# The norms of x on TensorE: turned blocks, squared from PSUM and summed by matmuls with a column of ones

## The chip, the cores and the metric

The kernel runs on one core of a Trainium2 chip. The metric is the device time of one execution, in microseconds (us); a smaller number is better.

## What is computed

The input x has 4096 rows of 128 numbers, and adj is a 4096 x 4096 matrix of zeros and ones. The first layer needs the norm of each row of x, the cosines between all rows, a softmax over them masked by adj, and two products with x; then come a layer norm, a second product with adj, a weight matrix, and another layer norm. The part that the change touches is the norm:

```python
norms = jnp.maximum(jnp.linalg.norm(x, axis=-1), COS_EPS)
sim = x @ x.T / (norms[:, None] * norms[None, :])
attn = jax.nn.softmax(beta * sim * adj, axis=1)
...
return diffusion + jax.nn.sigmoid(alpha) * (attn @ x - x)
```

## The kernel before

The rows of x are held as 32 blocks of 128 rows (`x_keep`), loaded by four DMAs of 512 KB, each a quarter q of eight blocks (L238). Then SyncE's queue issues the pieces of adj (L242), and casts of them on ScalarE (L482) free their buffers again.

The opening of the program makes the unit rows, each row of x divided by its norm, turned so that the row's 128 numbers lie across the partitions. For a quarter q the steps are:

- ScalarE squares the quarter's numbers. Quarters 0 to 2 take one instruction each (`squares`, L457). Quarter 3 takes eight, one per block, and each of these also sums its own squares (`block_squares`, L467).
- VectorE sums the squares of quarters 0 to 2 (L655) and takes the larger of the sum and a floor (`norms2`, L658).
- ScalarE takes the root (`norm_root`, L474), VectorE the reciprocal (`rnorm`, L664).
- GpSimd multiplies the quarter by its reciprocals (`unit_rows`, L313), one quarter after another.
- TensorE transposes the unit rows, four blocks at a time (`turn_rows`, L991, eight groups g). ScalarE writes the upper half of each as fp16 (`turned_high`, L490), VectorE the rest (`xnt_low`, L668).

From all norms VectorE finds the largest in each partition (L681); TensorE turns that column (L1084), VectorE finds the largest of all (L689), TensorE spreads it to all partitions by a matmul with a column of ones (L1087), and VectorE makes scales of it (L692 to L695). GpSimd waits for these scales before it splits x into fp16 parts (`x_split`, L359).

Then the cosines start (L1007). Row blocks r = 0 to 31 follow, in a loop from r = 2 on: cosines on TensorE, masking with adj on VectorE (L708), exponentials on ScalarE (L523), transposes of them (L1018), products with x (L1040, L1043). The second part sums y and z with adj on TensorE (L1056, L1176, L1204).

Everything is written by hand: each engine has its own program, in which instructions run in the order written, and semaphores tie the engines together. TensorE's program of the opening is the list of calls from L1075 on. In it, `keep_busy(n)` issues n matmuls of the identity with itself, whose results nobody reads:

```python
keep_busy(24)
...
turn_rows(0)
turn_rows(1)
keep_busy(3)
turn_rows(2)
turn_rows(3)
keep_busy(5)
```

An fp32 matmul appears in the trace as two passes, each with a weight load and a matmul record; an fp32 transpose appears as one.

Of the kernel before, what the change touches and what calls it, by code (L numbers as in the profile page):

```python
# [26 lines left out]
ALU = mybir.AluOpType  # L27
ACT = mybir.ActivationFunctionType
AX = mybir.AxisListType
F32 = mybir.dt.float32  # L30
# [7 lines left out]
P = 128  # L38
# [10 lines left out]
MIN_NORM = 1e-8  # L49
# [3 lines left out]
def two_layer_gnn(nc, x, adj, alpha, beta, weights, out):  # L53
    N, D = x.shape
    R = N // P
# [3 lines left out]
    CH = 1024  # L59
    C = N // CH  # L60
    TC = CH // P
    H = N // BANK
    TH = BANK // P
# [11 lines left out]
    with ExitStack() as ctx:  # L75
        def sb(name, shape, dt):
            return ctx.enter_context(nc.sbuf_tensor(name, shape, dt))

        def psum(name, shape, dt):
            return ctx.enter_context(nc.psum_tensor(name, shape, dt))  # L80

        def sem(name):
            return ctx.enter_context(nc.semaphore(name))
# [5 lines left out]
        x_keep = sb("x_keep", [P, R, D], F32)  # L89
# [6 lines left out]
        u = sb("u", [P, R, D], F32)  # L96
# [3 lines left out]
        ident = sb("ident", [P, P], F32)  # L100
        col = sb("col", [P, 30], F32)
        packed = sb("packed", [P, 2, W], U32)
        norm2 = sb("norm2", [P, R, 2], F32)
        norm = sb("norm", [P, R], F32)
        norm_r = sb("norm_r", [P, R], F32)
        deg = sb("deg", [P, C, R], F32)
# [9 lines left out]
        def c(n):  # L116
            return col[:, n:n + 1]
        alpha_c, beta_c, e_alpha, sigma, _, abs_beta = (c(n) for n in range(6))
        neg_max = [c(6), c(29)]
        total, r_total, gain = (c(n) for n in range(7, 10))  # L120
        attn_scale, x_up, dif_scale, _, _, eps_c = (c(n) for n in range(10, 16))
        great, pow2, rpow2 = c(16), c(18), c(20)
        sign_beta, top = c(24), c(25)
        table_loads = [c(26), c(27), c(28)]
        rstd = sb("rstd", [P, G], F32)

        ps_s = psum("ps_s", [P, 2, BANK], F32)
        ps_e = psum("ps_e", [P, 4, BANK], F32)
        ps_acc = psum("ps_acc", [P, BANK], F32)
        ps_at = psum("ps_at", [P, BANK], F32)  # L130

        x_loaded = [sem(f"x_loaded{q}") for q in range(C)]
# [3 lines left out]
        land_full = [[sem(f"land_full{q}_{i}") for i in range(C)] for q in range(2)]  # L136
        ident_zero = sem("ident_zero")
        ident_done = sem("ident_done")
        squares_done = sem("squares_done")
        norms2_done = sem("norms2_done")  # L140
        root_done = sem("root_done")
        floor_set = sem("floor_set")
        dve_step = sem("dve_step")
        rnorm_done = sem("rnorm_done")
        xn_done = [sem(f"xn_done{q}") for q in range(C)]
# [69 lines left out]
        zT = late[:, 0:2 * BANK].rearrange("p (a i) -> p a i", a=2)  # L215
        early = scores[:, 1, :]
        zw_ps = [ps_acc, ps_at]
        attn_ps = [ps_acc[:, :], ps_e[:, 3, :]]
        sum_ps = [ps_s[:, 0, :], ps_s[:, 1, :], ps_e[:, 2, :], ps_e[:, 3, :]]
        ones = eT_parts[0:1, 1, 1, 0:2 * P].bitcast(F32)  # L220
# [81 lines left out]
        @block.gpsimd  # L302
        def _(pool):
            nc.gpsimd.memset(ones, 1.0)
            nc.gpsimd.memset(ident[:, :], 0.0).then_inc(ident_zero, 1)
            pool.wait_ge(ident_zero, 1)
            nc.gpsimd.affine_select(out=ident[:, :], in_=ident[:, :], compare_op=ALU.not_equal, fill=1.0, base=0,
# [144 lines left out]
        @block.scalar  # L452
        def _(act):

            def squares(q):
                act.wait_ge(x_loaded[q], 16)
                nc.scalar.activation(early[:, q * CH:(q + 1) * CH],  # L457
                                     x_keep[:, q * TC:(q + 1) * TC, :].rearrange("p r d -> p (r d)"),
                                     ACT.Square).then_inc(squares_done, 1)

            def block_squares(q, a):

                if a == 0:
                    act.wait_ge(floor_set, 1)
                    act.wait_ge(x_loaded[q], 16)
                for r in range(q * TC + a * TC // 2, q * TC + (a + 1) * TC // 2):
                    ins = nc.scalar.activation(early[:, r * P:(r + 1) * P], x_keep[:, r, :], ACT.Square,  # L467
                                               accum_out=norm2[:, r, 0:1])
                if a == 1:
                    ins.then_inc(squares_done, 1)  # L470

            def norm_root(q):
                act.wait_ge(norms2_done, q + 1)
                nc.scalar.activation(norm[:, q * TC:(q + 1) * TC], norm[:, q * TC:(q + 1) * TC], ACT.Sqrt,  # L474
                                     scale=1.0 / (XN_SCALE * XN_SCALE)).then_inc(root_done, 1)
# [12 lines left out]
            def turned_high(g):  # L488
                act.wait_ge(xnt_turned, g + 1)
                nc.scalar.activation(xn_parts[:, 0, g * BANK:(g + 1) * BANK], ps_e[:, g % 4, :],  # L490
                                     ACT.Copy).then_inc(xnt_hi, 1)

            squares(0)
            squares(1)
            norm_root(0)
            squares(2)
            norm_root(1)
            block_squares(3, 0)
            turned_high(0)
            norm_root(2)  # L500
            block_squares(3, 1)
            turned_high(1)
            norm_root(3)
            turned_high(2)
# [132 lines left out]
        def _(dve):  # L637
            steps = [0]

            def link(ins):  # L640

                steps[0] += 1
                ins.then_inc(dve_step, 1)
                dve.wait_ge(dve_step, steps[0])
# [1 line left out]
            nc.vector.memset(eps_c, LN_EPS).then_inc(eps_set, 1)  # L646

            nc.vector.memset(top, 0.0)
            nc.vector.memset(norm2[:, :, 1:2], MIN_NORM * MIN_NORM).then_inc(floor_set, 1)

            def norms2(q):

                dve.wait_ge(squares_done, q + 1)
                if q < C - 1:
                    link(nc.vector.tensor_reduce(norm2[:, q * TC:(q + 1) * TC, 0],  # L655
                                                 early[:, q * CH:(q + 1) * CH].rearrange("p (r d) -> p r d", d=D),
                                                 AX.X, ALU.add))
                nc.vector.tensor_reduce(norm[:, q * TC:(q + 1) * TC], norm2[:, q * TC:(q + 1) * TC, :], AX.X,  # L658
                                        ALU.max).then_inc(norms2_done, 1)

            def rnorm(q):

# [312 lines left out]
        def _(pe):  # L975
            pe.wait_ge(ident_done, 1)
            def keep_busy(n):

                for _ in range(n):
                    nc.tensor.matmul(ps_acc[:, 0:P], ident[:, :], ident[:, :], start=True, stop=True)  # L980

            keep_busy(24)

            def turn_rows(g):

                pe.wait_ge(xn_done[g // 2], 1)
                if g >= 4:
                    pe.wait_ge(xnt_lo, g - 3)
                for n in range(TH):
                    t = TH * g + SLOT[n]  # L990
                    ins = nc.tensor.transpose(ps_e[:, g % 4, n * P:(n + 1) * P], early[:, t * P:(t + 1) * P],  # L991
                                              ident[:, :])
                ins.then_inc(xnt_turned, 1)
# [67 lines left out]
            def row(r, q, second=False):  # L1061

                for h in range(H):
# [8 lines left out]
                    else:  # L1072
                        attend(r - 1, 1 - q, h + H - LAG, second, order=range(H) if second else ATTEND_ORDER)

            turn_rows(0)  # L1075
            turn_rows(1)
            keep_busy(3)
            turn_rows(2)
            turn_rows(3)
            keep_busy(5)  # L1080
            turn_rows(4)
            turn_rows(5)
            pe.wait_ge(great_done, 1)
# [4 lines left out]
                             start=True, stop=True).then_inc(great_spread, 1)  # L1088
# [165 lines left out]
```

## Time and profile before

| what | us |
|---|---|
| median of 3 runs | 655.35 |
| lowest and highest run | 654.85, 655.55 |
| the profiled execution's own time | 654.72 |
| its span, first to last instruction | 652.9 |
| TensorE busy | 638.8 (98% of the span) |
| VectorE busy | 516.7 (79%) |
| ScalarE busy | 412.6 (63%) |
| GpSimd busy | 237.4 (36%) |

The span is 1.8 us shorter than the execution's own time, which also holds what lies around the first and last instruction. Busy time counts all stretches together. The change lies in the first 18 us, and what TensorE's program does there is seen in the timeline and not in the shares.

### The profile page before, as it was taken

How to read it: one execution, taken by the hardware profiler on the slowest of the kernel's cores; microseconds unless marked ns; L12 is line 12 of the kernel's file. 1: busy time of each engine (PE TensorE's matmuls, PEld its weight loads, DVE VectorE, ACT ScalarE, POOL GpSimd, SP SyncE). 2: the span in 40 equal slices, each digit the busy share in tenths (PEclk: the TensorE clock that was granted, in tenths of full speed). 3: DMA queues.
4: the chain of work that ended last, by engine and by line, in shares of the span. 5: the costliest groups of instructions: out<-in, count | busy, mean ns of one | idle time of the engine just before them, and what ended most of it. 6: DMA issues, size and time to landing. Idle time of an engine off the chain costs nothing.

```text
span 652.9 us, 16141 instructions
## 1 busy us (share of the span) xinstructions
PE 638.8 (98%) x5103; PEld 465.8 (71%) x5103; DVE 516.7 (79%) x1565; ACT 412.6 (63%) x768; POOL 237.4 (36%) x249
## 2 busy tenths in 40 slices
PE   8889999999999999999999999999999999999996
PEld 7456777777777777777777777888888864444465
DVE  5989999999999999999999998887777863334453
ACT  7999999999999999999999998611111110000000
POOL 5999644544544544644644647300000000000000
PEclk9999999999999999999999999999999999999999
DMA  7879999999999999999999995300000000000001
GB/s 278 310 162 256 298 236 246 289 252 244 292 251 234 297 247 251 306 241 248 299 239 251 289 252 95 73 7 0 0 0 0 0 1 1 17 16 18 16 32 33
DMA packets 165020, 107.37 MB, mean 164 GB/s; under 512 B 144384, under 2 KB 148608, under 8 KB 164992
## 3 DMA queue, kind: packets, MB, share of 16 engines
q1 hardware_dynamic: 164992, 107.04, 62.7%
q8 instruction: 12, 0.20, 0.1%
q14 instruction: 16, 0.13, 0.1%
HBM read 69.27 MB, written 2.10 MB: 109 GB/s over the span
## 4 chain that ended last, share of the span: by engine, by line
PE 90%; DVE 3%; ACT 2%; DMA 2%; issue 1%; POOL 1%; SPq 0%; DVEq 0%; ACTq 0%; POOLq 0%
PE ps_s L1007 23%; PE ps_s L1204 17%; PE ps_e L1176 15%; PE ps_acc L1040 8%; PE ps_e L1018 8%; PE ps_e L1040 8%; PE ps_acc L1043 4%; PE ps_e L1043 4%; DMA x_keep<-in_x 1%; DMA eTx<-e_parts 1%; DVE scores L708 1%; PE ps_e L1056 1%; ACT scores L523 1%; DVE y_parts L819 1%; PE ps_s L1056 1%
## 5 line engine op out<-in xcount | busy, mean ns | idle before, releaser
L1007 PE MATMUL ps_s<-xn_parts,xn_signed 128*128 128x512 f16 x756 | 203.3, 379 | 2.9 <-DVE cmax L708 2.9
L708 DVE CUSTOM_DVE_ANT_1 scores<-ps_s,adj_bytes 128x512 f32<-128x512 f32 x252 | 171.8, 684 | 22.3 <-PE ps_s L1007 15.3
L523 ACT ACTIVATE scores<-scores,col 128x1024 f32<-128x1024 f32 x128 | 157.3, 1232 | 1.1 <-DVE col L719 0.9
L482 ACT ACTIVATE adj_bytes<-land 128x1024 uint8<-128x1024 f32 x128 | 133.5, 1047 | 0.6 <-POOL packed L343 0.6
L351 POOL TENSOR_SCALAR e_parts<-scores 128x1024 f16<-128x1024 f32 x64 | 68.5, 1071 | 152.9 <-ACT scores L523 149.4
L1176 PE MATMUL ps_e<-y_parts,stage 128*128 128x256 f16 x896 | 98.0, 273 | 0.0
L1007 PEld LDWEIGHTS ps_s<-xn_parts,xn_signed 128*128 128x128 f16 x756 | 68.5, 98 | 38.5 <-DVE cmax L708 2.5
L1176 PEld LDWEIGHTS ps_e<-y_parts,stage 128*128 128x128 fp8e4 x896 | 87.7, 98 | 10.1
L530 ACT ACTIVATE eT_parts<-ps_e 128x512 f16<-128x512 f32 x128 | 75.9, 596 | 26.2 <-PE ps_e L1018 25.0
L723 DVE SCALAR_TENSOR_TENSOR eT_parts<-ps_e,eT_parts 128x512 f16<-128x512 f32 x128 | 87.3, 684 | 1.9 <-ACT eT_parts L530 1.9
L729 DVE SCALAR_TENSOR_TENSOR e_parts<-scores,e_parts 128x1024 f16<-128x1024 f32 x64 | 86.3, 1350 | 0.4 <-POOL e_parts L351 0.4
L1018 PE MATMUL ps_e<-ident,scores 128*128 128x128 f32 x512 | 77.0, 274 | 0.8 <-ACT scores L523 0.8
L619 ACT ACTIVATE scores<-ps_s 128x512 f32<-128x512 f32 (+1 forms) x9 | 4.9, 550 | 108.6 <-PE ps_s L1204 108.6
L596 ACT ACTIVATE std<-mv,col 128x1 f32<-128x1 f32 x32 | 9.4, 295 | 84.2 <-DVE mv L900 84.2
L1204 PE MATMUL ps_s<-stage,x_parts 128*128 128x512 fp8e4 (+1 forms) x320 | 56.9, 336 | 0.0
L1204 PE MATMUL ps_s<-land,x_parts 128*128 128x512 fp8e4 x256 | 56.4, 379 | 0.0
L1018 PEld LDWEIGHTS ps_e<-ident,scores 128*128 128x128 f32 x512 | 53.9, 140 | 3.0 <-DVE eT_parts L723 0.8
L805 DVE TENSOR_SCALAR stage<-packT 128x256 uint32<-128x256 uint32 (+1 forms) x192 | 42.6, 286 | 12.5 <-PE ps_e L1176 12.3
L1040 PE MATMUL ps_acc<-x_parts,eT_parts 128*128 128x256 f16 x256 | 49.1, 273 | 1.6 <-DVE eT_parts L723 1.6
L340 POOL TENSOR_TENSOR packed<-packed,adj_bytes 128x256 uint32<-128x256 uint32 x48 | 49.4, 1029 | 2.7
L1040 PE MATMUL ps_acc<-x_parts,eTx 128*128 128x256 f16 x256 | 48.9, 273 | 0.5 <-DMA eTx<-e_parts 0.5
L1040 PE MATMUL ps_e<-x_parts,eT_parts 128*128 128x256 f16 x256 | 48.9, 273 | 0.0
(128 smaller groups left out, 972.2 us busy)
## 6 DMA issues: line engine op xcount, KB each, us to landing
land<-in_adj SPq DMA_DIRECT2D x128, 512.0 KB, 5.4
x_keep<-in_x SPq DMA_DIRECT2D x4, 512.0 KB, 5.6
out<-u SPq DMA_DIRECT2D x7, 256.0 KB, 2.1
eTx<-e_parts SPq DMA_TRANSPOSE x64, 4.3
packT<-packed SPq DMA_TRANSPOSE x16, 7.0
out<-u SPq DMA_DIRECT2D x2, 128.0 KB, 1.7
scores<-in_L_gnn_weights SPq DMA_DIRECT2D x1, 64.0 KB, 1.9
col<-in_L_gnn_beta SPq DMA_DIRECT2D x1, 0.5 KB, 7.2
```

The costliest lines, as they stand in the source:

```text
L351: nc.gpsimd.tensor_scalar(e_parts[:, n, 0, :], scores[:, q, (n + 2) * CH:(n + 3) * CH], E_SCALE, 1.0, ALU.mult, ALU.mult).wait_op(sign_don ...
L482: nc.scalar.activation(adj_bytes[:, q, i * CH:(i + 1) * CH], land[:, q, i, :], ACT.Copy, scale=float(BYTE_TOP[q] >> i), accum_out=deg[:, i ...
L523: nc.scalar.activation(piece, piece, ACT.Exp, bias=neg_max[q], scale=abs_beta, accum_out=csum[:, q, i:i + 1]).then_inc(exp_done, 1)
L530: nc.scalar.activation(eT_parts[:, b, 0, :], ps_e[:, b % 2, :], ACT.Copy, scale=E_SCALE).then_inc(e_hi, 1)
L708: nc.vector.tensor_tensor_reduce(scores[:, q, o:o + BANK].rearrange("p (k q) -> p k q", k=K), score_bank(h, r == 0 if start else False).re ...
L723: nc.vector.scalar_tensor_tensor(eT_parts[:, b, 1, :], ps_e[:, b % 2, :], E_SCALE, eT_parts[:, b, 0, :], ALU.mult, ALU.subtract).then_inc( ...
L729: nc.vector.scalar_tensor_tensor(e_parts[:, n, 1, :], scores[:, q, (n + 2) * CH:(n + 3) * CH], E_SCALE, e_parts[:, n, 0, :], ALU.mult, ALU ...
L1007: ins = nc.tensor.matmul(score_bank(h, start), xn_signed[:, q, part, :], xn_parts[:, other, o:o + BANK], start=(part == 0 and other == 0), ...
L1018: ins = nc.tensor.transpose(ps_e[:, b % 2, n * P:(n + 1) * P], scores[:, q, t * P:(t + 1) * P], ident[:, :])
L1040: nc.tensor.matmul(attn_ps[q][:, 0:2 * D], hi, x_parts[:, t, :], start=(k == 0 and n == 0), stop=(k == H - 1 and n == TH - 1), skip_group_ ...
L1176: ins = nc.tensor.matmul(ps_e[:, n, 0:2 * D], stage8[n][:, b, :, k], y_tiles[t], start=(t == 0), stop=(t == R - 1))
L1204: ins = nc.tensor.matmul(ps_s[:, q, 0:rows * P], x_parts[:, t, part * D:(part + 1) * D], quads8[q if rows == G else 1][:, b, k, n:n + rows ...
```

## The change

The squares of x are no longer taken from x itself. TensorE transposes the raw blocks of x, four at a time, into PSUM (`turn_raw`); ScalarE squares the turned blocks from PSUM into `u` (`raw_squares`); TensorE multiplies each squared block with a column of ones, which sums over the partitions and leaves the squared norms of 128 rows as one column in PSUM (`sum_norms`); VectorE only takes the larger of sum and floor (`norms2`). VectorE's sums and ScalarE's eight single blocks of quarter 3 go, as does the table of floors. The column of ones is set by GpSimd at the start. Eight groups g of four blocks replace the four quarters of the squares. `keep_busy` falls from 24 to 8 at the start, and calls of 2, 2, 3 and 3 stand between the new steps.

```diff
...
-        norm2 = sb("norm2", [P, R, 2], F32)
...
+        one = c(13)
...
+        one_set = sem("one_set")
+        raw_turned = sem("raw_turned")
+        norms_summed = sem("norms_summed")
-        floor_set = sem("floor_set")
...
+        norm_ps = ps_at[:, 3 * P:3 * P + R]
...
+            nc.gpsimd.memset(one, 1.0).then_inc(one_set, 1)
...
         @block.scalar
         def _(act):
-            def squares(q):
-                act.wait_ge(x_loaded[q], 16)
-                nc.scalar.activation(early[:, q * CH:(q + 1) * CH],
-                                     x_keep[:, q * TC:(q + 1) * TC, :].rearrange("p r d -> p (r d)"),
+            def raw_squares(g):
+
+                act.wait_ge(raw_turned, g + 1)
+                nc.scalar.activation(u[:, TH * g:TH * g + TH, :].rearrange("p n d -> p (n d)"), ps_s[:, g % 2, :],
                                      ACT.Square).then_inc(squares_done, 1)
-
-            def block_squares(q, a):
-
-                if a == 0:
-                    act.wait_ge(floor_set, 1)
-                    act.wait_ge(x_loaded[q], 16)
-                for r in range(q * TC + a * TC // 2, q * TC + (a + 1) * TC // 2):
-                    ins = nc.scalar.activation(early[:, r * P:(r + 1) * P], x_keep[:, r, :], ACT.Square,
-                                               accum_out=norm2[:, r, 0:1])
-                if a == 1:
-                    ins.then_inc(squares_done, 1)
             def norm_root(q):
                 act.wait_ge(norms2_done, q + 1)
...
                 nc.scalar.activation(xn_parts[:, 0, g * BANK:(g + 1) * BANK], ps_e[:, g % 4, :],
                                      ACT.Copy).then_inc(xnt_hi, 1)
-            squares(0)
-            squares(1)
+            raw_squares(0)
+            raw_squares(1)
+            raw_squares(2)
             norm_root(0)
-            squares(2)
+            raw_squares(3)
             norm_root(1)
-            block_squares(3, 0)
+            raw_squares(4)
+            raw_squares(5)
             turned_high(0)
             norm_root(2)
-            block_squares(3, 1)
+            raw_squares(6)
+            raw_squares(7)
             turned_high(1)
             norm_root(3)
             turned_high(2)
...
             nc.vector.memset(eps_c, LN_EPS).then_inc(eps_set, 1)
             nc.vector.memset(top, 0.0)
-            nc.vector.memset(norm2[:, :, 1:2], MIN_NORM * MIN_NORM).then_inc(floor_set, 1)
             def norms2(q):
-                dve.wait_ge(squares_done, q + 1)
-                if q < C - 1:
-                    link(nc.vector.tensor_reduce(norm2[:, q * TC:(q + 1) * TC, 0],
-                                                 early[:, q * CH:(q + 1) * CH].rearrange("p (r d) -> p r d", d=D),
-                                                 AX.X, ALU.add))
-                nc.vector.tensor_reduce(norm[:, q * TC:(q + 1) * TC], norm2[:, q * TC:(q + 1) * TC, :], AX.X,
-                                        ALU.max).then_inc(norms2_done, 1)
+                dve.wait_ge(norms_summed, q + 1)
+                nc.vector.tensor_scalar(norm[:, q * TC:(q + 1) * TC], norm_ps[:, q * TC:(q + 1) * TC],
+                                        MIN_NORM * MIN_NORM, None, ALU.max).then_inc(norms2_done, 1)
             def rnorm(q):
...
                 for _ in range(n):
                     nc.tensor.matmul(ps_acc[:, 0:P], ident[:, :], ident[:, :], start=True, stop=True)
-            keep_busy(24)
+            keep_busy(8)
+
+            def turn_raw(g):
+
+                pe.wait_ge(x_loaded[g // 2], 16)
+                if g >= 2:
+                    pe.wait_ge(squares_done, g - 1)
+                for n in range(TH):
+                    ins = nc.tensor.transpose(ps_s[:, g % 2, n * P:(n + 1) * P], x_keep[:, TH * g + n, :], ident[:, :])
+                ins.then_inc(raw_turned, 1)
+
+            def sum_norms(g):
+
+                if g == 0:
+                    pe.wait_ge(one_set, 1)
+                if g >= 2:
+                    pe.wait_ge(norms2_done, g // 2)
+                pe.wait_ge(squares_done, g + 1)
+                for t in range(TH * g, TH * g + TH):
+                    ins = nc.tensor.matmul(norm_ps[:, t:t + 1], u[:, t, :], one, start=True, stop=True)
+                if g % 2 == 1:
+                    ins.then_inc(norms_summed, 1)
             def turn_rows(g):
...
                     else:
                         attend(r - 1, 1 - q, h + H - LAG, second, order=range(H) if second else ATTEND_ORDER)
+            turn_raw(0)
+            turn_raw(1)
+            keep_busy(2)
+            sum_norms(0)
+            turn_raw(2)
+            sum_norms(1)
+            turn_raw(3)
+            keep_busy(2)
+            sum_norms(2)
+            sum_norms(3)
+            keep_busy(3)
+            turn_raw(4)
+            turn_raw(5)
             turn_rows(0)
             turn_rows(1)
-            keep_busy(3)
+            sum_norms(4)
+            sum_norms(5)
+            turn_raw(6)
+            turn_raw(7)
             turn_rows(2)
             turn_rows(3)
-            keep_busy(5)
+            sum_norms(6)
+            sum_norms(7)
+            keep_busy(3)
             turn_rows(4)
             turn_rows(5)
             pe.wait_ge(great_done, 1)
...
```

TensorE's program, before, from its first matmul to the last transposes of unit rows (L980 is `keep_busy`, L991 `turn_rows`, L1084 and L1087 the turning and the spreading of the largest norm):

```order
L980 MATMUL ps_acc<-ident 128x128 x24
L991 MATMUL ps_e<-ident,scores 128x128 x8
L980 MATMUL ps_acc<-ident 128x128 x3
L991 MATMUL ps_e<-ident,scores 128x128 x8
L980 MATMUL ps_acc<-ident 128x128 x5
L991 MATMUL ps_e<-ident,scores 128x128 x8
L1084 MATMUL ps_at<-ident,col 1x128
L980 MATMUL ps_acc<-ident 128x128 x3
L1087 MATMUL ps_at<-col,eT_parts 128x1
L991 MATMUL ps_e<-ident,scores 128x128 x8
```

The four quarters of unit rows are the only work here besides the filler and the largest norm.

The same place in the changed program, first half (L971 is `keep_busy`, L981 `turn_raw`, L992 `sum_norms`, L1003 `turn_rows`):

```order
L971 MATMUL ps_acc<-ident 128x128 x8
L981 MATMUL ps_s<-ident,x_keep 128x128 x8
L971 MATMUL ps_acc<-ident 128x128 x2
L992 MATMUL ps_at<-col,u 128x1 x4
L981 MATMUL ps_s<-ident,x_keep 128x128 x4
L992 MATMUL ps_at<-col,u 128x1 x4
L981 MATMUL ps_s<-ident,x_keep 128x128 x4
L971 MATMUL ps_acc<-ident 128x128 x2
L992 MATMUL ps_at<-col,u 128x1 x8
L971 MATMUL ps_acc<-ident 128x128 x3
L981 MATMUL ps_s<-ident,x_keep 128x128 x8
L1003 MATMUL ps_e<-ident,scores 128x128 x8
```

The first transposes of unit rows (L1003), which stood right behind the filler, now stand behind six groups of raw transposes and four groups of sums.

And the second half, to the turning of the largest norm (L1114, before L1084):

```order
L992 MATMUL ps_at<-col,u 128x1 x8
L981 MATMUL ps_s<-ident,x_keep 128x128 x8
L1003 MATMUL ps_e<-ident,scores 128x128 x8
L992 MATMUL ps_at<-col,u 128x1 x8
L971 MATMUL ps_acc<-ident 128x128 x3
L1003 MATMUL ps_e<-ident,scores 128x128 x8
L1114 MATMUL ps_at<-ident,col 1x128
```

The sums of quarter 3 are the last L992 row, behind the unit rows of quarter 1, which stand in the second L1003 row counting from the top.

ScalarE, before, from its first squares to the last root (L457 and L467 are squares, L474 roots, L490 `turned_high`):

```order
L457 ACTIVATE scores<-x_keep 128x1024 x2
L474 ACTIVATE norm<-norm 128x8
L457 ACTIVATE scores<-x_keep 128x1024
L474 ACTIVATE norm<-norm 128x8
L467 ACTIVATE scores,norm<-x_keep 128x128 x4
L490 ACTIVATE xn_parts<-ps_e 128x512
L474 ACTIVATE norm<-norm 128x8
L467 ACTIVATE scores,norm<-x_keep 128x128 x4
L490 ACTIVATE xn_parts<-ps_e 128x512
L474 ACTIVATE norm<-norm 128x8
```

and with the change (L462 is `raw_squares`, L467 the root, L483 `turned_high`):

```order
L462 ACTIVATE u<-ps_s 128x512 x3
L467 ACTIVATE norm<-norm 128x8
L462 ACTIVATE u<-ps_s 128x512
L467 ACTIVATE norm<-norm 128x8
L462 ACTIVATE u<-ps_s 128x512 x2
L483 ACTIVATE xn_parts<-ps_e 128x512
L467 ACTIVATE norm<-norm 128x8
L462 ACTIVATE u<-ps_s 128x512 x2
L483 ACTIVATE xn_parts<-ps_e 128x512
L467 ACTIVATE norm<-norm 128x8
```

Each L462 row reads PSUM that a `turn_raw` has written, so ScalarE's squares now wait for TensorE instead of a DMA.

## Rows read from the trace of the kernel before

**Rows 1.** The chain that ended last, 2 to 18 us: start, us, what.
```profile
2.31 7.44 DMA x_keep<-in_x
9.84 1.28 ACT scores L467 x8
...
11.70 1.17 ACT scores L467 x8
...
16.64 1.02 PE ps_e L991 x8
```
**Rows 2.** Busy time by stretch, all engines: PE, PEld, DVE, ACT, POOL, PEclk, DMA share, GB/s.
```profile
17.50:55.00 37.50, 32.26 (x228) 19.92 (x225) 34.19 (x89) 35.84 (x66) 35.56 (x38) 1.00 0.83 234
60.00:400.00 340.00, 339.99 (x2887) 249.36 (x2885) 316.61 (x821) 317.36 (x556) 176.14 (x189) 1.00 1.00 258
```
**Rows 3.** Timeline: start us, us, engine line op [idle before]; GpSimd, ScalarE, VectorE around the norms.
```profile
7.37 1.90 POOL L313 TENSOR_TENSOR scores<-x_keep,norm_r 128x1024 f32<-128x1024 f32 x1 [5.76 <-DVE norm_r L664]
12.02 3.75 POOL L313 TENSOR_TENSOR scores<-x_keep,norm_r 128x1024 f32<-128x1024 f32 x2 [0.21 <-DVE norm_r L664]
17.55 1.12 POOL L359 TENSOR_SCALAR u<-x_keep,col 128x1024 f32<-128x1024 f32 x1 [0.64 <-DVE col L695]
...
13.48 0.20 DVE L664 RECIPROCAL norm_r<-norm 128x8 f32<-128x8 f32 x1 [0.41 <-ACT norm L474]
...
4.29 1.06 ACT L457 ACTIVATE scores<-x_keep 128x1024 f32<-128x1024 f32 x1 [2.06 <-DMA x_keep<-in_x]
6.63 0.17 DVE L658 TENSOR_REDUCE norm<-norm 128x8 f32<-128x16 f32 x1
6.83 0.21 ACT L474 ACTIVATE norm<-norm 128x8 f32<-128x8 f32 x1
7.08 0.20 DVE L664 RECIPROCAL norm_r<-norm 128x8 f32<-128x8 f32 x1 [0.28 <-ACT norm L474]
...
17.27 1.08 ACT L490 ACTIVATE xn_parts<-ps_e 128x512 f16<-128x512 f32 x2 [0.85 <-PE ps_e L991]
```
**Rows 4.** Group of one line, 0 to 17.6 us: count, busy, mean ns, idle before it.
```profile
L655 DVE TENSOR_REDUCE norm<-scores 128x8 f32<-128x1024 f32 x3 | 3.6, 1185 | 4.4 <-ACT scores L457 4.4
```
**Rows 5.** TensorE alone by stretch from 1.60: length, busy (instructions begun), PEclk, DMA share, GB/s.
```profile
1.60:2.31 0.71, 0.66 (x3) 1.00 0.58 82
1.60:5.21 3.61, 3.56 (x16) 1.00 0.95 299
1.60:5.31 3.71, 3.65 (x17) 1.00 0.94 296
1.60:7.01 5.41, 5.36 (x29) 1.00 0.91 287
1.60:9.01 7.41, 7.36 (x47) 1.00 0.88 281
```
**Rows 6.** Timeline of TensorE and its weight loads, 9 to 31 us.
```profile
12.79 1.28 PE L980 MATMUL ps_acc<-ident 128*128 128x128 f32 x10
16.27 0.38 PE L1087 MATMUL ps_at<-col,eT_parts 1*128 1x1 f32 x2 [0.42 <-DVE col L689]
16.58 1.09 PE L991 MATMUL ps_e<-ident,scores 128*128 128x128 f32 x8
16.27 0.29 PEld L1087 LDWEIGHTS ps_at<-col,eT_parts 1*128 1x128 f32 x2 [0.61 <-DVE col L689]
...
30.75 0.22 PE L1043 MATMUL ps_acc<-x_parts,eT_parts 128*128 128x128 f16 x1
30.81 0.27 PE L1040 MATMUL ps_acc<-x_parts,eT_parts 128*128 128x256 f16 x1
```
**Rows 7.** One line, L1087: ns min/median/max, first and last start.
```profile
L1087 PEld LDWEIGHTS ps_at<-col,eT_parts x2: 181/182/184, 16.3 to 16.4; 1*128 1x128 f32 x2
L1087 PE MATMUL ps_at<-col,eT_parts x2: 245/256/266, 16.3 to 16.4; 1*128 1x1 f32 x2
```
**Rows 8.** VectorE's first read of what L1087 left in PSUM (timeline).
```profile
16.74 0.14 DVE L692 TENSOR_SCALAR col<-ps_at 128x1 f32<-128x1 f32 x1
```

## The prediction

> **What bounds the kernel now.** I read the chain of waits first, then the busy times by stretch, then the timeline of the opening engine by engine. The chain [rows 1] shows the opening as one line of work: the last quarter of x lands at 2.31 + 7.44 = 9.75 us, ScalarE squares its blocks in two halves, and VectorE's norms and the search for the largest of them follow. GpSimd's unit rows (1.90 us a quarter) run until 12.02 + 3.75 = 15.77 us [rows 3]. From 16.64 us TensorE turns the last unit rows, and about 17.5 the cosines start.
>
> What a delay of that point costs is seen in [rows 2]. Between 60 and 400 us TensorE is busy 339.99 of 340 us, so a later start is not made up there. Between 17.5 and 55 us VectorE, ScalarE and GpSimd are each busy 34 to 36 of 37.5 us, and GpSimd's part begins with the scales of the largest norm, at 17.55 [rows 3]. All three hang on the opening. So **a microsecond in the opening is a microsecond in the result**, and I look for the time at which the last quarter's reciprocals (L664, 13.48 us [rows 3]) start after the change; what follows them is the same on every engine.
>
> **What a pass of TensorE costs.** The new program of the opening is long on TensorE, so its passes are priced first. At the start 17 - 3 = 14 passes begin between about 2.25 and 5.25 us, some 0.214 us apart; 16 have begun by 5.21 and the 17th by 5.31. By 7.01 us 29 have begun and by 9.01 us 47, which is 0.111 apart [rows 5]. The clock column says 1.00 throughout, but the first spacing is that of the lower level (1.2 GHz) and the second that of the higher (2.4 GHz); the change of pace lies near 6 us, after four microseconds of unbroken filler.
> - A filler pass costs 0.112 at the higher level: ten take 1.28 us, of which the last one's 0.275 is drain [rows 6].
> - A transpose costs (1.09 - 0.275) / 7 = 0.115, so four cost 0.46 [rows 6].
> - A sum matmul loads 128 columns of fp32 weights and streams one column. No row shows that at full depth. The nearest is L1087, also fp32, also two passes, 128 columns of weights and one moving column, but one partition deep: two loads take 0.29 us together and one takes 0.181 to 0.184, so the second began 0.108 after the first [rows 6, 7]. The lower bound is an fp16 pass of 128 moving columns with its own load, 30.81 - 30.75 = 0.06 at most [rows 6]. I take 0.108, since dtype, column count and width are the sums' own. Four matmuls are eight passes: 0.87 us a group, 6.9 us for all eight groups (64 passes). At 0.055 it would be 3.5 us.
>
> The Trainium skill ("TensorE: Matmul & The Clock Gate", section "LDWEIGHTS (loading the stationary operand)") says that a load's time goes with its columns and not with its depth, and gives columns / 1.2 ns, which is 107 for 128; the next section says that the fast load is not had with fp32. By that the sums cost what L1087 shows and the fp16 bound falls away; by the fp16 row the total below would be 3.4 us smaller. The trace's 108 ns agrees at depth one; no row shows depth 128.
>
> **The change step by step.** I follow TensorE's new program from 1.66 us, where its filler begins.
> 1. `keep_busy(8)` is 16 passes at the low pace: until 5.23 us, where the 17th pass started before [rows 5]. x's first quarter has landed by then (ScalarE squared it from 4.29 us on [rows 3]), but TensorE is not free.
> 2. The first four raw transposes take the places of passes 17 to 20, until about 6.06. From there on each pass is at the high pace if the clock rises as before.
> 3. From 6.06 to the end of the last sums there are 28 raw transposes, 16 of unit rows (44 x 0.115 = 5.06 us), 14 filler passes (1.57) and 64 sum passes (6.91): 13.54 us, ending at 19.60. The waits on the way: ScalarE starts to square 0.69 us after four transposes begin (17.27 - 16.58, [rows 3, 6]) and takes 0.58, so squares are there 1.27 us after their transposes start; the sums of group 4, for instance, come up at 14.31 and have had squares since 13.73, group 6 at 17.88 since 17.30. The unit rows of quarters 0 and 1 are ready at 12.04 and 14.66 and asked for at 13.39 and 16.96. No wait is late: **TensorE is the bound from 1.66 to 19.60**.
> 4. The last sum pass begins at 19.49; add 0.36 (L1087's second start, 16.38, to VectorE's read of its result at 16.74 [rows 7, 8]): VectorE takes the floor at 19.85. The root follows 0.20 and the reciprocal 0.25 later, by the spacing of 6.63, 6.83 and 7.08 us [rows 3]. The reciprocals start at **20.30 us instead of 13.48: 6.8 us late**.
>
> What it saves is VectorE's three sums, 3.6 us [rows 4], and eight single squares on ScalarE. Neither buys anything here. VectorE's sum of quarter 3 was not on VectorE before, and both engines now wait for TensorE. The memset of the ones on GpSimd lies under the filler.
>
> Behind the reciprocals everything keeps its distances. GpSimd multiplies quarter 3 from 20.59 to 22.47, and the last transposes, 6.8 us late, ask for it at 23.40; before, it was ready at 15.77 and used at 16.58 [rows 3, 6]. The pieces of adj land as early as before, but none of the steps between 17.5 and 55 us in the chain was waiting for one, so being early buys nothing. The price of 6.8 us comes through whole: 654.72 + 6.8 = 661.5 for an execution like the profiled one, which lies 0.6 below the median of the runs, so **662.1 us** as a median.
>
> **The rivals.**
> - *Cheap loads.* The sum passes cost 0.055 as in fp16, the reciprocals start at about 16.9 and the time is 655.35 + 3.4 = 658.8. For it speaks that a load can lie under a stream; against it that the sums have nothing but one column to lie under, and L1087's own spacing.
> - *The sums hide: not slower.* The 64 loads run ahead under the transposes and the sums take no time of TensorE's own. Then TensorE is no longer the bound: it would wait for the unit rows, whose 1.90 us a quarter now follow a first reciprocal near 8.5 us, and turns quarter 1 at about 12.6. The last sums end near 13.5 and the reciprocals start at 14.2, 0.7 late: 656.0, within the 0.2% (1.3 us) that a measurement of this kernel can tell from no change. The point from which it decides is a group of sums at 0.16 us of TensorE: its program then ends at 19.60 - 6.91 + 8 x 0.16 = 13.97, and the reciprocals start 1.2 late. Against it: two back-to-back loads in L1087 did not overlap. Faster is hardly open: the last quarter lands at 9.75, and four steps behind it (transposes 0.69, square 0.58, one group of sums 1.1 with its drain, floor and root 0.45) put the reciprocals at 12.6 at best, 0.9 before today's, with TensorE free at that time, which it is not.
> - *The clock falls.* The sums stream one column per pass, so TensorE's array does little in half of the stretch from 7 to 20 us, and the pace may fall back to that of the first passes. Each ten passes then cost 1.0 us more; if it held from the first sums to the last, about 110 passes, 11 us come on top: 673. If it held for a third of them, 666. For it: the start shows that the low pace exists [rows 5]. Against it: between 11 and 16.6 us before, with TensorE idle at times [rows 6], the passes kept 0.112 apart.
>
> The Trainium skill (same page, "A second HAM failure mode: psum-queue depth-cycling") tells of a kernel whose TensorE paused briefly between groups until its clock kept falling; by that this rival would be the outcome. No row here shows a fall while TensorE still issues, so it keeps a small chance.
> - *Not what it says.* If the filler of 8 already ran at the high pace, x's first landing would hold TensorE back instead and some 1 us would come off: 661. That stays inside the forecast.
>
> **How the numbers follow.** TensorE-bound with sums of 0.095 to 0.125 a pass, 661 to 663.5: 0.68. Cheap or half-cheap loads, 657.5 to 661: 0.14. The clock falls: 0.10. The sums hide, or the delay is absorbed by something that I don't see: 0.06 about even, 0.02 faster. The likeliest is 662.1. The range takes the forecast, the cheap loads from 657.6 up and a short fall of the clock up to 665.5. Faster by over 0.2% 0.02, within 0.2% 0.06, slower 0.92.
>
> **What would show it.** In the changed profile the sum passes should stand 0.108 apart, TensorE should be without a gap from 1.66 to about 19.6 us, the first unit rows on GpSimd start near 10.1 instead of 7.37, the fourth reciprocal near 20.3, the cosines near 24.3, and from there each step 6.8 us later than before. Reciprocals before 17 us would refute the price of a sum pass; a late start and an unchanged time would refute that the opening is paid in full; spacings of 0.21 after 7 us would show the clock.

## The result and the profile after

The changed kernel takes 662.15 us (median of 5 runs, 661.65 to 663.1) against 655.35 (median of 5 runs in the same comparison). The ratio is 1.0103, with a 95% interval of 1.0092 to 1.0114: 6.0 to 7.5 us slower. The prediction was 662.1.

The timeline of TensorE in the changed kernel (start us, us, engine, line, tiles, count) shows its program one piece behind the other; some pieces are left out here:

```profile
1.68 3.78 PE L971 MATMUL ps_acc<-ident 128*128 128x128 f32 x16 [1.68 <-POOL ident L311]
5.26 1.47 PE L981 MATMUL ps_s<-ident,x_keep 128*128 128x128 f32 x8
...
7.07 1.02 PE L992 MATMUL ps_at<-col,u 128*128 128x1 f32 x8
...
17.85 1.84 PE L992 MATMUL ps_at<-col,u 128*128 128x1 f32 x16
19.55 0.92 PE L971 MATMUL ps_acc<-ident 128*128 128x128 f32 x6
...
24.19 1.46 PE L1019 MATMUL ps_s<-xn_parts,xn_signed 128*128 128x512 f16 x6
```

The last 16 sum passes (L992) begin at 17.85 and the next piece at 19.55: 1.70 / 16 = 0.106 us a pass. The cosines (L1019) start at 24.19, where they started at 17.50 before: 6.69 us later.

Busy time by stretch (PE, PEld, DVE, ACT, POOL, PEclk, DMA share, GB/s), from the first sum to the last, and in the row loop:

```profile
7.07:19.55 12.48, 12.48 (x115) 12.48 (x115) 1.67 (x7) 5.31 (x12) 5.69 (x3) 1.00 0.87 343
66.70:406.70 340.00, 340.00 (x2889) 249.59 (x2887) 317.98 (x820) 317.29 (x556) 175.34 (x187) 1.00 1.00 258
```

TensorE has not a moment free in the first stretch, at a granted clock of 1.00, while VectorE is busy for 1.67 of 12.48 us. The second row answers to [rows 2]: the loop is as full as before.

The waits from 0 to 24 us (who waited for whom, us in total, times, longest) and the timeline of the reciprocals and of GpSimd's unit rows:

```profile
DVE norm L649 <- PE ps_at L992: 16.3, 4, 8.5
POOL scores L317 <- DVE norm_r L655: 13.1, 4, 8.5
ACT u L462 <- PE ps_s L981: 6.1, 3, 4.1
```
```profile
19.73 0.17 DVE L649 TENSOR_SCALAR norm<-ps_at 128x8 f32<-128x8 f32 x1 [2.29 <-PE ps_at L992]
20.17 0.20 DVE L655 RECIPROCAL norm_r<-norm 128x8 f32<-128x8 f32 x1 [0.28 <-ACT norm L467]
...
10.14 1.90 POOL L317 TENSOR_TENSOR scores<-x_keep,norm_r 128x1024 f32<-128x1024 f32 x1 [8.51 <-DVE norm_r L655]
```

All three engines end up waiting for TensorE, GpSimd by way of VectorE's reciprocals. The fourth reciprocal starts at 20.17 us (13.48 before, [rows 3]), and the first unit rows at 10.14 (7.37 before).

### The profile page after: what moved, and what is told of

Its sections match the earlier page's. It is cut to its first block, busy times and chain, and to the rows that moved or that the text cites. A ratio compares the mean times of both kernels' runs of the same rounds, so it can differ in the third digit from the quotient of the medians.

```text
span 660.2 us, 16275 instructions
## 1 busy us (share of the span) xinstructions
PE 646.1 (98%) x5171; PEld 473.1 (72%) x5171; DVE 515.3 (78%) x1561; ACT 411.6 (62%) x757; POOL 237.7 (36%) x250
## 4 chain that ended last, share of the span: by engine, by line
PE 88%; DMA 2%; DVE 2%; ACT 1%; issue 0%; SPq 0%; DVEq 0%; ACTq 0%
PE ps_s L1019 23%; PE ps_s L1234 17%; PE ps_e L1206 15%; PE ps_e L1052 8%; PE ps_e L1030 8%; PE ps_acc L1052 8%; PE ps_e L1055 4%; PE ps_acc L1055 4%; DMA eTx<-e_parts 2%; DVE e_parts L720 1%; PE ps_e L1068 1%; PE ps_acc L1218 1%; PE ps_at L1218 0%; ACT y_parts L566 0%; PE ps_s L1068 0%
## 5 line engine op out<-in xcount | busy, mean ns | idle before, releaser
L1019 PE MATMUL ps_s<-xn_parts,xn_signed 128*128 128x512 f16 x756 | 203.3, 379 | 2.9 <-DVE cmax L699 2.9
L1019 PEld LDWEIGHTS ps_s<-xn_parts,xn_signed 128*128 128x128 f16 x756 | 68.6, 98 | 38.2 <-DVE cmax L699 2.5
L720 DVE SCALAR_TENSOR_TENSOR e_parts<-scores,e_parts 128x1024 f16<-128x1024 f32 x64 | 90.0, 1408 | 0.0
L1052 PE MATMUL ps_e<-x_parts,eTx 128*128 128x256 f16 x256 | 49.0, 273 | 1.3 <-DMA eTx<-e_parts 1.3
```

Of the source, the lines that this page charges most:

```text
L720: nc.vector.scalar_tensor_tensor(e_parts[:, n, 1, :], scores[:, q, (n + 2) * CH:(n + 3) * CH], E_SCALE, e_parts[:, n, 0, :], ALU.mult, ALU ...
L1019: ins = nc.tensor.matmul(score_bank(h, start), xn_signed[:, q, part, :], xn_parts[:, other, o:o + BANK], start=(part == 0 and other == 0), ...
L1052: nc.tensor.matmul(attn_ps[q][:, 0:2 * D], hi, x_parts[:, t, :], start=(k == 0 and n == 0), stop=(k == H - 1 and n == TH - 1), skip_group_ ...
```

## The experiments

**One pass per sum.** The squares and the column of ones become fp16, so a sum matmul is one pass with an fp16 load.

```diff
-        one = c(13)
+        one = c(13).bitcast(F16)[:, 0:1]
+        sq16 = u[:, :, :].rearrange("p n d -> p (n d)").bitcast(F16)
...
-                nc.scalar.activation(u[:, TH * g:TH * g + TH, :].rearrange("p n d -> p (n d)"), ps_s[:, g % 2, :],
+                nc.scalar.activation(sq16[:, BANK * g:BANK * (g + 1)], ps_s[:, g % 2, :],
...
-                    ins = nc.tensor.matmul(norm_ps[:, t:t + 1], u[:, t, :], one, start=True, stop=True)
+                    ins = nc.tensor.matmul(norm_ps[:, t:t + 1], sq16[:, t * P:(t + 1) * P], one, start=True, stop=True)
```

Expected: 

> The changed kernel with the squares written as fp16 and a column of ones in fp16, so a sum matmul is one pass with an fp16 load. Theory (TensorE's own program is the bound, and the fp32 loads of the sums are its largest part): 32 passes near 0.06 us take the place of 64 at 0.106; TensorE then waits a little for squares and for unit rows; the fourth reciprocal starts near 15.5 us instead of 20.17 and the time falls by 4 to 5 us, to about 657.5. Rival (the way over PSUM and ScalarE and the waits between the engines set the end, whatever a sum pass costs): reciprocal near 20 us, 661.5 to 662.5.

Measured: 656.74 us, ratio to the kernel before 1.0021 (1.001 to 1.0033). In the timeline the eight sum passes of quarter 3 and the fourth reciprocal:

```profile
14.30 0.36 PE L993 MATMUL ps_at<-col,u 128*128 128x1 f16 x8
...
15.14 0.20 DVE L656 RECIPROCAL norm_r<-norm 128x8 f32<-128x8 f32 x1 [0.27 <-ACT norm L468]
```

and over the whole run (ns min/median/max of one pass):

```profile
L993 PE MATMUL ps_at<-col,u x32: 163/163/167, 7.6 to 14.5; 128*128 128x1 f16 x32
```

The reciprocal comes 5.0 us earlier than in the change, and the median falls by 5.4: the sum passes were the larger part of the loss. Eight passes take 0.36 us, of which 0.163 is one pass's own duration, so they start (0.36 - 0.163) / 7 = 0.028 apart, a quarter of the fp32 ones.

**A late start by itself.** The kernel before, with `keep_busy(5)` raised to `keep_busy(35)`.

```diff
-            keep_busy(5)
+            keep_busy(35)
```

Expected: 

> The kernel before with 30 more filler matmuls (60 passes, 6.7 us) ahead of the unit rows of quarter 2, and nothing else changed: a delay of the opening by itself. Theory (a microsecond in the opening is a microsecond in the result): the cosines start about 6 us later (some 0.7 of the 6.7 is taken back since VectorE has finished its fp16 parts of groups 2 and 3 by then), and the end is later by the same amount, about 661.4. Rival (the rows make up for part of a late start): less than 4 us later, under 659.5.

Measured: 662.65 us, ratio 1.0105 (1.0086 to 1.0125), 7.3 us over the kernel before. The filler and the cosines in its timeline:

```profile
13.60 7.98 PE L980 MATMUL ps_acc<-ident 128*128 128x128 f32 x70
...
24.40 1.46 PE L1007 MATMUL ps_s<-xn_parts,xn_signed 128*128 128x512 f16 x6
```

The cosines are 6.90 us late, and the end as much or a little more (the profiled execution's span is 660.7 us against 652.9). Nothing of the delay is made up in the 630 us behind it. In this execution the third quarter of x also landed 0.8 us later than in the profile before (ScalarE squares it from 9.25 us and not from 8.44, ahead of the second quarter's root, so the second quarter's unit rows came later too), which is why the 6.7 us of filler moved the cosines by more than 6.

**What VectorE's sums were worth.** The kernel before, with the three sums reading 16 of the 128 squares of a row.

```diff
-                                                 early[:, q * CH:(q + 1) * CH].rearrange("p (r d) -> p r d", d=D),
+                                                 early[:, q * CH:(q + 1) * CH].rearrange("p (r d) -> p r d", d=D)[:, :, 0:16],
```

Expected: 

> The kernel before with VectorE's three sums cut to 16 of 128 squares (the norms of quarters 0 to 2 leave out seven eighths of the squares). It shows what the change's saving on VectorE is worth by itself. Theory (VectorE's sums are on no path that sets the end): the fourth reciprocal stays within 0.3 us of 13.48 and the time within 0.5 us of 655.35. Rival (the saving is real and is paid for by the rest of the change): 654 or less.

Measured: 655.42 us, ratio 0.9993 (0.9982 to 1.0004). The timeline of quarter 3's first square and last reciprocal:

```profile
9.31 0.31 ACT L467 ACTIVATE scores<-x_keep 128x128 f32<-128x128 f32 x1 [0.30 <-DMA x_keep<-in_x]
...
12.95 0.20 DVE L664 RECIPROCAL norm_r<-norm 128x8 f32<-128x8 f32 x1 [0.41 <-ACT norm L474]
```

The reciprocal is 0.53 us earlier, but so is the landing of x. From the first square to the reciprocal it is 12.95 - 9.31 = 3.64 us, and in the kernel before 13.48 - 9.84 = 3.64 as well [rows 1, 3]. The three sums take 0.23 to 0.29 us each here, where they took 1.2 [rows 4], and the median is the same: the sums lay on no path that sets the end, and shortening them is worth nothing.

**No filler between the sums.** The changed kernel without the calls of 2, 2 and 3.

```diff
             turn_raw(1)
-            keep_busy(2)
...
             turn_raw(3)
-            keep_busy(2)
             sum_norms(2)
             sum_norms(3)
-            keep_busy(3)
```

Expected: 

> The changed kernel without the seven filler matmuls between the raw transposes and the sums (14 passes, 1.57 us). Theory (TensorE is the bound from 1.66 us to the last sums): the fourth reciprocal comes 1.2 to 1.4 us earlier (a little of the gap is taken by the wait for the first squares), about 660.8. Rival one (the waits set the end): no change, 662. Rival two (the filler holds the clock up): passes 0.21 us apart in part of the stretch from 7 to 20 us, 664 or more.

Measured: 669.42 us (664.26 to 671.09), ratio 1.0182 (1.0132 to 1.0232). Less work for the engine that bounds, and 7 us more. Its busy times by stretch show why (columns as above):

```profile
10.00:12.00 2.00, 2.00 (x16) 1.98 (x14) 0.20 (x1) 0.70 (x2) 1.58 (x1) 0.76 0.71 277
12.00:14.00 2.00, 2.00 (x11) 2.00 (x11) 0.37 (x2) 0.55 (x2) 0.89 (x2) 0.50 1.04 424
20.00:22.00 2.00, 2.00 (x11) 2.00 (x10) 0.62 (x2) 1.37 (x3) 1.85 (x1) 0.50 0.40 160
28.00:32.00 4.00, 4.00 (x22) 3.68 (x21) 2.56 (x9) 1.68 (x4) 1.90 (x3) 0.56 0.42 131
```

TensorE is busy throughout, yet its granted clock falls within the sixteen sum passes that begin at 9.99 and stays at 0.50 (1.2 GHz) until after 28 us. Sixteen sum passes then take twice as long:

```profile
9.99 2.68 PE L992 MATMUL ps_at<-col,u 128*128 128x1 f32 x16
...
15.97 3.41 PE L992 MATMUL ps_at<-col,u 128*128 128x1 f32 x16
19.25 1.95 PE L981 MATMUL ps_s<-ident,x_keep 128*128 128x128 f32 x8
```

That is (19.25 - 15.97) / 16 = 0.205 us a pass. Rival two of the expectation is what happened.

**Only the two calls of two gone.** As above, but with the call of three kept.

```diff
             turn_raw(1)
-            keep_busy(2)
...
             turn_raw(3)
-            keep_busy(2)
```

Expected: 

> The changed kernel without the two calls of two filler matmuls, but with the call of three ahead of the raw transposes of quarter 2. All fillers between the sums gone: the clock fell to 0.5 at 11.5 us and the time rose by 7. One theory: the stretch of sums that has no filler ahead of it (the sixteen passes from 10.16 us) is what lets it fall, so it falls here as well, at about the same time, 664 to 671. The other: the filler of three right behind these sums holds it, and the gain of 0.5 us shows, about 661.6.

Measured: 665.54 us (665.19 to 666.21), ratio 1.0161 (1.0144 to 1.0178). TensorE by stretch (length, busy, clock, DMA share, GB/s):

```profile
8.00:9.00 1.00, 1.00 (x12) 1.00 0.49 154
9.00:9.50 0.50, 0.50 (x5) 0.60 0.20 54
10.00:12.00 2.00, 2.00 (x12) 0.50 0.73 289
14.00:16.00 2.00, 2.00 (x12) 0.52 1.02 416
16.00:18.00 2.00, 2.00 (x21) 1.00 1.02 418
```

Its timeline at the fall:

```profile
8.21 0.95 PE L992 MATMUL ps_at<-col,u 128*128 128x1 f32 x8
9.02 1.04 PE L981 MATMUL ps_s<-ident,x_keep 128*128 128x128 f32 x4
9.85 3.41 PE L992 MATMUL ps_at<-col,u 128*128 128x1 f32 x16
```

The clock falls again, and the time is where the first theory put it, but the place is another: between 9.0 and 9.5 us, in four raw transposes (1.04 us, where the change takes 0.63), before the sixteen sums begin at 9.85. Up to the end of these sums TensorE's program is the same as without any filler, and there the fall came some 2 us later. So the sixteen sums without a filler ahead of them are not what lets the clock fall here; which of the passes before them do is not shown. The clock is back at 1.00 by 16 us, after the filler of three and during eight transposes. That the filler brought it back is likely and not shown: one of the four runs without any filler (664.26 us, mean granted clock 0.994) lies near these four (0.991 to 0.995).

**A shorter filler at the start.**

```diff
-            keep_busy(8)
+            keep_busy(4)
```

Expected: 

> The changed kernel with 4 filler matmuls at the start instead of 8: TensorE is free when x's first quarter lands, at about 4.3 us, and is idle for some 0.8 us before it. Theory (TensorE is the bound from its first raw transposes on): the first sums start about 0.65 us earlier than at 7.07 and so does everything behind them, 661.5. Rival (TensorE's pace hangs on what it did before, and fewer passes at the start let it rise later or fall again, as it fell when the fillers between the sums were taken away): passes 0.21 us apart well after 7 us, a granted clock of 0.5 in a stretch, 664 or more.

Measured: runs of 662.02, 662.85, 668.89 and 674.57 us, a median of 665.87; the ratio without the slowest is 1.0143 (1.009 to 1.0195). The profiled execution is the slowest of the four, so its numbers are one case and not the usual one:

```profile
4.26 1.97 PE L981 MATMUL ps_s<-ident,x_keep 128*128 128x128 f32 x8 [0.50 <-DMA x_keep<-in_x]
...
20.74 3.41 PE L992 MATMUL ps_at<-col,u 128*128 128x1 f32 x16
24.01 1.95 PE L981 MATMUL ps_s<-ident,x_keep 128*128 128x128 f32 x8
```
```profile
20.00:22.00 2.00, 2.00 (x12) 1.00 0.35 139
```

TensorE starts 1.0 us earlier on x, but its sums are still 0.204 us apart at 20.74: in this execution the pace had not risen by then. The clock column (the second row: length, busy, clock, DMA share, GB/s) reads 1.00 here, as it did for the slow first passes of the kernel before [rows 5]; the spacing tells it, the column doesn't. The rival holds for this execution. Two of the other runs lie where the theory put them or little above, so the shorter filler makes the time uncertain; no run is faster than the change's fastest (661.63).

**Wide sums, no filler.** Again no filler between the sums, but each sum matmul streams 96 columns of ones.

```diff
-        one = c(13)
+        WIDE = 96
+        one = eTx[:, 0, 0, 0:2, :].rearrange("p a j -> p (a j)").bitcast(F32)[:, 0:WIDE]
...
-        norm_ps = ps_at[:, 3 * P:3 * P + R]
+        norm_ps = ps_at[:, 3 * P:4 * P]
...
-                    ins = nc.tensor.matmul(norm_ps[:, t:t + 1], u[:, t, :], one, start=True, stop=True)
+                    ins = nc.tensor.matmul(norm_ps[:, t:t + WIDE], u[:, t, :], one, start=True, stop=True)
```

Expected: 

> The changed kernel without the seven filler matmuls between the sums (as where the clock fell to 0.5 at 11.5 us and the time went to 669), but each sum matmul streams 96 columns of ones instead of one; the later ones overwrite all but the column that counts. Theory one (a sum pass is priced by its load): passes stay 0.106 to 0.115 us apart although they stream 96 times as much. Theory two (one-column passes let the clock fall, though TensorE issues without a gap; passes that stream do not): no stretch at 0.5, the fourth reciprocal 1.2 to 1.4 us before 20.17, time about 660.8. Rival (the clock falls for the weight loads, the waits, or for want of the fillers as such): a granted clock of 0.5 again, 664 or more.

Measured: 662.32 us, ratio 1.0116 (1.0099 to 1.0133). Its timeline:

```profile
5.30 1.04 PE L982 MATMUL ps_s<-ident,x_keep 128*128 128x128 f32 x8
...
9.36 2.05 PE L993 MATMUL ps_at<-eTx,u 128*128 128x96 f32 x16
11.24 1.04 PE L982 MATMUL ps_s<-ident,x_keep 128*128 128x128 f32 x8
...
16.49 1.92 PE L993 MATMUL ps_at<-eTx,u 128*128 128x96 f32 x16
18.25 0.86 PE L972 MATMUL ps_acc<-ident 128*128 128x128 f32 x6
...
18.89 0.20 DVE L656 RECIPROCAL norm_r<-norm 128x8 f32<-128x8 f32 x1 [0.27 <-ACT norm L468]
```

From the sixteen passes at 9.36 to the next piece it is 11.24 - 9.36 = 1.88 us, 0.118 a pass, and from the last sixteen 18.25 - 16.49 = 1.76 us, 0.11 a pass. That is at most 0.012 over the 0.106 of the change: 96 columns cost nearly what one column costs, so the streamed columns do not set the price of a pass. What is left is its load, whose records fill 12.48 of 12.48 us in the change. The granted clock is 1.00 in every stretch from 8 to 20 us. The mean granted clock of whole runs says the same of the executions without a trace: 0.996 to 0.999 in ten runs of the wide sums (these four and six below), 0.981 to 0.994 in the four with one column and no filler. The reciprocal is 1.28 us earlier than in the change, as the theory had it, though in part for another reason: the pace rose earlier, so the first eight raw transposes take 1.04 us, where the change takes 1.47. The median, however, did not fall.

**Both once more.** To see whether the 1.28 us are lost on the way, the wide sums and the change ran again together.

Expected of the wide sums: 

> The wide sums without filler a second time, more rounds: its opening was 1.28 us shorter than the change's, yet its median the same, and its profile shows 1.9 us lost later, in waits of TensorE for DMA transposes. Theory (those waits differ from run to run and have nothing to do with the opening): its median lies 0.5 to 1.5 us under that of the change in the same call. Rival (the earlier start is lost to the transposes each time): the two medians within 0.3 us.

Expected of the change: 

> The change itself, for the same chip and call: fourth reciprocal near 20.17 us, opening 6.7 us late, median 661.5 to 662.5; the waits for DMA transposes after 250 us, 1.2 us in its first profile and 0.5 in that of the kernel before, should come out at another number if they differ from run to run.

Measured: 661.74 us for the wide sums (661.58 to 663.45) and 662.98 for the change (661.63 to 663.6); ratios 1.010 (1.0082 to 1.0118) and 1.0113 (1.0095 to 1.0131). The fourth reciprocals and, of the change, the first raw transposes:

```profile
18.79 0.20 DVE L656 RECIPROCAL norm_r<-norm 128x8 f32<-128x8 f32 x1 [0.28 <-ACT norm L468]
```
```profile
5.26 1.92 PE L981 MATMUL ps_s<-ident,x_keep 128*128 128x128 f32 x8
...
20.68 0.20 DVE L655 RECIPROCAL norm_r<-norm 128x8 f32<-128x8 f32 x1 [0.28 <-ACT norm L467]
```

The change missed its expectation: its reciprocal came at 20.68, 0.5 us later than in its first profile, since the pace rose later (the eight raw transposes take 1.92 us, and 1.47 there), and its median lies above 662.5. The waits of TensorE for DMA transposes from 250 us on were, in the first profiles of the wide sums and of the change (us, times, longest):

```profile
PE ps_e L1053 <- DMA eTx<-e_parts: 1.7, 3, 0.9
```
```profile
PE ps_e L1052 <- DMA eTx<-e_parts: 0.4, 1, 0.4
```

In the second profiles they are 1.7 and 0.3. So the waits came back in each kernel and are not chance from run to run, as I had held. The medians now differ by 1.24, as the theory had it, but the lowest runs are level (661.58 and 661.63), the ranges overlap, and the first medians (662.32 and 662.15) did not differ that way. In the profiled executions the earlier start is mostly lost: the reciprocals start at 18.89 and 18.79 (wide) and at 20.17 and 20.68 (the change), and the spans are 660.2 and 659.8, and 660.2 and 660.2. From the fourth reciprocal to the end the wide sums take 641.3 and 641.0 us, the change 640.1 and 639.5, the kernel before 639.5 and the fp16 sums, which also wait for DMA transposes (1.4 us), 641.4. So how much of a gain of one or two microseconds reaches the end, and what sets these waits, stays open.

**The shortest way in this order.** fp16 sums, four fillers at the start, one call of two between the sums.

```diff
-            keep_busy(8)
+            keep_busy(4)
...
             turn_raw(3)
-            keep_busy(2)
             sum_norms(2)
             sum_norms(3)
-            keep_busy(3)
```

(from the kernel with fp16 sums)

Expected: 

> The fp16 sums with 4 filler matmuls at the start, and without the filler ahead of sums 2 and ahead of the raw transposes of quarter 2: the shortest way through TensorE that this order of work allows. Theory: the fourth reciprocal near 14.1 us instead of 15.14, about 655.8, level with the kernel before and not under it, since the last quarter of x lands near 9.8 us and its transposes, squares, sums and root follow. Rival (the clock): fewer passes and more waits let it fall, 659 or more.

Measured: 657.49 us (655.34 to 659.23), ratio 1.0033 (1.0013 to 1.0054).

```profile
8.18 1.09 PE L982 MATMUL ps_s<-ident,x_keep 128*128 128x128 f32 x4
...
13.87 1.07 PE L982 MATMUL ps_s<-ident,x_keep 128*128 128x128 f32 x8
...
16.49 0.20 DVE L656 RECIPROCAL norm_r<-norm 128x8 f32<-128x8 f32 x1 [0.28 <-ACT norm L468]
```

Four transposes take 1.09 us at 8.18 and eight take 1.07 at 13.87: the pace rose only in between, and the reciprocal came at 16.49, later than with more filler (15.14). No version of the change has a median under that of the kernel before, whose last reciprocal comes 3.64 us after the first square of x's last quarter.

## Why the prediction was right

The steps of the prediction's working, one by one:

- *The first filler* was to end at 5.23 us; the raw transposes started at 5.26. TensorE was not free when x landed, as forecast.
- *The price of a sum pass* was taken as 0.108 us from L1087 [rows 6, 7]; it measured 0.106 over 16 passes. This was the term that decided between 6.8 and 3.4 us, and the row of the same dtype, column count and width was the right one to take. The bound from the fp16 row was not even a bound: one-column fp16 passes start 0.028 apart. The wide sums show that the number of streamed columns hardly matters to an fp32 pass. A slip beside it changes little: (1.09 - 0.275) / 7 is 0.116 and not 0.115, which makes 0.06 us over the 44 transposes.
- *TensorE as the bound* was to last until 19.60, with no wait late; it lasted until 19.55, without a gap.
- *The end of the chain* was to be the fourth reciprocal at 20.30, 6.8 us late; it was 20.17, 6.7 late. The cosines were forecast near 24.3 and started at 24.19. That it came so close is partly luck: the pace rose near 6 us, where one profile of the kernel before had it, and in the second profile of the change it rose later and the reciprocal came at 20.68.
- *A microsecond for a microsecond*: the filler put into the kernel before showed it for a delay of this size, 6.90 us at the cosines and 7.3 in the median. For a difference of one or two microseconds the wide sums don't bear it out: 1.3 and 1.9 us at the reciprocal were 0.0 and 0.4 in the spans.
- *VectorE's saving worth nothing*: shown by the shortened sums, the same median and 3.64 us from square to reciprocal either way.

Two things in it were weaker than they looked. The profiled execution's span grew by 660.2 - 652.9 = 7.3 us, 0.6 more than the cosines' delay; the rest came at the end of the row loop, where a wait for a DMA transpose of 0.4 us stands that the kernel before does not have at that place. The medians differ by 6.8, so the sum met them to better than its steps allow.

And the rival of the falling clock was argued away with the wrong row. I held against it that the passes kept their pace before, although TensorE idled at times. That says nothing of a TensorE that issues all the time and streams one column a pass. The experiments show how near the change is to it: without two calls of two fillers the clock falls. The fillers, which I counted as 1.57 us of cost, go with a pace that holds: without all of them, or without two of the three calls, it fell. The remark under *Not what it says*, that a first filler at the higher pace would save 1 us, is untouched by this, but the shortening of that filler, which it may suggest, gained nothing: two runs stayed at 662.0 and 662.9, and the other two took 668.9 and 674.6.

## What to carry to other kernels

Before work is moved to a matrix engine, count its passes and price one by a row of the same dtype and the same number of weight columns: a sum over partitions by a column of ones pays the whole weight load for one column. A saving on an engine that waits anyway is worth nothing, and a delay of seven microseconds ahead of a full loop was paid whole here. When filler is taken out, look at the spacing of the passes behind it, in more than one execution, and not at the busy share.

## What the runs showed of the hardware that I had not expected

- TensorE's granted clock fell to 0.50 while TensorE was busy without a gap, among one-column fp32 sums and raw transposes: within sums that began at 9.99, until after 28 us (no filler), or within transposes that began at 9.02, until almost 16 us (filler of three kept). With 96 columns a pass, and no filler either, it stayed at 1.00.
- With half the filler at the start, the low pace lasted past 20 us in one execution (0.204 us a sum pass at 20.74 us), and the four runs of that kernel lie between 662.0 and 674.6 us.
- A one-column pass with 128 columns of weights costs 0.106 us in fp32 and 0.028 in fp16, a factor of four.
- The transposes by DMA far behind the opening hold TensorE up by 0.3 to 1.7 us in all in the profiles named above, by much the same amount in both profiles of one kernel and by another in another kernel, though the instructions there are the same. Why is open.
